# A fused Mamba and mixture-of-experts kernel on one core: a reordered tail, with gated products on GpSimd

## The reference

```python
h = concat([cls, patchify(x) @ W.T + b]) + pos          # then the text tokens behind it
# layer 2 (Mamba): h -> LN -> xz = h @ W_in ; causal conv ; silu ; delta, B, C ; scan over time
y = ys + xc * D
h2 = h + (y * silu(z)) @ W_out                           # "output projection"
# layer 3: a shared gated FFN over all rows, and experts for the 512 rows of an index
shared = LN(silu(x1) * x2) @ sw3.T + sb3
x_moe = x[index_b, index_t]
scores = sigmoid(x_moe @ eg_w.T + eg_b); top1 = argmax(scores + exp_bias)
h1 = einsum('md,ehd->meh', x_moe, ew1) + eb1
h2 = einsum('md,ehd->meh', x_moe, ew2) + eb2
z  = LN(silu(h1) * h2)
out = einsum('meh,edh->med', z, ew3) + eb3               # all 8 experts; the top one is taken
final.at[index_b, index_t].set(shared_w * shared + expert_w * out[top1])
```

## Time and profile before

| | |
|---|---|
| median of 3 runs | 1708.54 us (1707.23 to 1710.84) |
| profiled execution | 1710.15 us |
| its span in the trace | 1708.0 us |
| busy: TensorE, VectorE, ScalarE, GpSimd | 87%, 90%, 78%, 92% of the span |
| last scan of the loop begins | at 1620.44 us |
| last TensorE instruction begins its group | at 1699.34 us |

### The profile page before, as it was taken

How to read it: one execution, slowest core, us unless ns; L and a number is a source line. 1 busy time by engine, 2 the same in 40 slices (tenths; PEclk the granted TensorE clock), 3 DMA queues, 4 the chain that set the end, 5 groups by cost and what they waited for, 6 DMA issues and landing times.

```text
span 1708.0 us, 28038 instructions
## 1 busy us (share of the span) xinstructions
PE 1483.6 (87%) x9868; PEld 1065.3 (62%) x9868; DVE 1544.3 (90%) x1389; ACT 1328.5 (78%) x3100; POOL 1563.2 (92%) x782
## 2 busy tenths in 40 slices
PE   8778898899889988898888898988988889896688
PEld 7656666666666666666666666666666666664355
DVE  2499999999999999999999999999999999999944
ACT  2577788888888888888888888888888888887644
POOL 0599999999999999999999999999999999999914
PEclk8888999999999999999999999999999999997899
DMA  4667755566667555666665556666655566566110
GB/s 136 143 126 178 182 127 124 121 133 140 136 137 152 125 124 117 137 142 138 135 153 125 121 120 137 142 137 136 153 125 122 123 133 142 121 143 140 39 35 16
DMA packets 194430, 218.47 MB, mean 128 GB/s; under 512 B 94011, under 2 KB 184773, under 8 KB 193778
## 3 DMA queue, kind: packets, MB, share of 16 engines
q1 hardware_dynamic: 193522, 215.51, 56.9%
q0 software_dynamic: 576, 1.17, 0.3%
q10 hardware_dynamic: 192, 0.01, 0.0%
HBM read 169.92 MB, written 47.09 MB: 127 GB/s over the span
## 4 chain that ended last, share of the span: by engine, by line
DVE 24%; POOL 19%; ACT 18%; issue 13%; PE 12%; DMA 12%; SPq 2%; DVEq 0%; ACTq 0%; POOLq 0%
DVE psum L1317 12%; POOL xr L1664 12%; ACT psum L1020 7%; DMA u<-u_scratch 7%; DVE xr L1317 5%; DVE xr L1326 5%; PE psum L620 4%; DMA u_scratch<-u 4%; POOL u L1685 3%; ACT L1142 2%; POOL xr L1672 2%; ACT L1051 2%; PE psum L792 2%; SPq L482 2%; ACT soft L1068 2%
## 5 line engine op out<-in xcount | busy, mean ns | idle before, releaser
L1664 POOL TENSOR_TENSOR xr<-u,bbc 128x912 f32<-128x912 f32 x512 | 1076.3, 2137 | 13.7 <-DMA u<-u_scratch 13.7
L1020 ACT ACTIVATE psum<-delta,a_neg 128x228 f32<-128x228 f32 x2048 | 804.9, 440 | 199.4 <-DVE xr L1326 159.3
L1317 DVE TENSOR_TENSOR_SCAN psum<-psum,xr 128x912 f32<-128x912 f32 x320 | 654.3, 2045 | 10.6 <-POOL xr L1664 7.4
L1672 POOL TENSOR_TENSOR xr<-xr,cbc 128x912 f32<-128x912 f32 x192 | 409.3, 2132 | 35.7 <-DVE xr L1317 32.7
L1317 DVE TENSOR_TENSOR_SCAN xr<-psum,xr 128x912 f32<-128x912 f32 x192 | 393.3, 2048 | 31.3 <-ACT psum L1020 31.3
L1326 DVE TENSOR_TENSOR xr<-psum,cbc 128x912 f32<-128x912 f32 x320 | 352.2, 1101 | 3.8
L721 PE MATMUL psum<-xr,fold 128*32 128x228 f32 x4096 | 294.7, 385 | 30.3 <-POOL xr L1672 16.6
L620 PE MATMUL psum<-xh,win 128*128 128x228 f32 x1024 | 222.9, 367 | 41.0 <-ACT xs L1051 31.6
L620 PEld LDWEIGHTS psum<-xh,win 128*128 128x128 f32 x1024 | 192.6, 193 | 68.4 <-ACT xs L1051 41.9
L671 PE MATMUL psum<-xi,conv_d 128*128 128x228 f32 x1024 | 211.2, 358 | 0.0
L671 PEld LDWEIGHTS psum<-xi,conv_d 128*128 128x128 f32 x1024 | 190.5, 189 | 16.3 <-issue 11.7
(11 more groups left out here) (204 smaller groups left out, 1590.4 us busy)
## 6 DMA issues: line engine op xcount, KB each, us to landing
delta<-delta_scratch SPq DMA_DIRECT2D x256, 228.0 KB, 6.6
u<-u_scratch SPq DMA_DIRECT2D x256, 228.0 KB, 4.4
bbc<-bc_scratch SPq DMA_DIRECT2D x128, 114.0 KB, 2.6
u_scratch<-u SPq DMA_DIRECT2D x64, 228.0 KB, 4.1
cbc<-bc_scratch SPq DMA_DIRECT2D x128, 114.0 KB, 2.8
delta_scratch<-delta SPq DMA_DIRECT2D x64, 226.0 KB, 6.3
out<-ob SPq DMA_DIRECT2D x32, 228.0 KB
h_scratch<-h SPq DMA_DIRECT2D x31, 228.0 KB
```

Of the source, the lines that this page charges most:

```text
L1020: ins = nc.scalar.activation(slot(k)[:, j * TOK:(j + 1) * TOK], delta4[:, c // 2, j, c % 2], ACT.Exp, scale=a_neg[:, c, j, n:n + 1])
L1317: nc.vector.tensor_tensor_scan(x if k in on_pool(i) else slot(k), slot(k), x, 0.0, ALU.mult, ALU.add).then_inc(scan_done, 1)
L1664: nc.gpsimd.tensor_tensor(xr[:, k % XRING], u4[:, c // 2, :, c % 2], bbc[:, p, n].unsqueeze(1).to_broadcast([P, J, TOK]), ALU.mult).then_i ...
L1672: nc.gpsimd.tensor_tensor(xr[:, k % XRING], xr[:, k % XRING], cbc[:, p, k % NI].unsqueeze(1).to_broadcast([P, J, TOK]), ALU.mult).then_inc ...
```

## The change

The last output projection becomes two parts: `out_first` (behind unit 13 of group 31) and `out_second` (where `out_proj` was), in bank CB. The feed-forward work of group 31 goes to bank BB. `bias_rows` goes ahead of unit 10 into bank BB, and VectorE's addition to it goes from `after_last` to behind unit 12. TensorE's, VectorE's and ScalarE's orders of the expert part are rewritten. `gated` of blocks 0 to 2 goes from VectorE to GpSimd, where `shared_rows` goes ahead of `rstd_of(0)`.

```diff
-            h2_ps = psum[0:T, AB, 0:SEQ * DM].rearrange("p (s d) -> p s d", s=SEQ)
+            def h2_ps(g):
+                return psum[0:T, CB if g == GROUPS - 1 else AB, 0:SEQ * DM].rearrange("p (s d) -> p s d", s=SEQ)
...
-                return {GROUPS - 2: 2, GROUPS - 1: 3}.get(g, AB)
+                return {GROUPS - 2: 2, GROUPS - 1: BB}.get(g, AB)
...
+                    def out_first():
+                        g = GROUPS - 1
+                        pe.wait_ge(sz_done, 2 * GROUPS)
+                        pe.wait_ge(y_done, CH // 2 * g + 1)
+                        for s in range(SEQ):
+                            for k in range(DC):
+                                pe.matmul(h2_ps(g)[:, s, k * P:(k + 1) * P], h0[:, g % HRING, k, s * T:(s + 1) * T], ident[:],
+                                          start=(s == 0 and k == 0), stop=False)
+                            for c in range(CH // 2):
+                                pe.matmul(h2_ps(g)[:, s], y[:, g % 2, c, s * T:(s + 1) * T], wout[:, c], start=False, stop=False)
+                    def out_second():
+                        g = GROUPS - 1
+                        pe.wait_ge(y_done, CH // 2 * GROUPS)
+                        for s in range(SEQ):
+                            for c in range(CH // 2, CH):
+                                mm = pe.matmul(h2_ps(g)[:, s], y[:, g % 2, c, s * T:(s + 1) * T], wout[:, c],
+                                               start=False, stop=(s == SEQ - 1 and c == CH - 1))
+                        mm.then_inc(h2_mm, 1)
...
 (h2_turn)
+                        if g == GROUPS - 2:
+                            pe.wait_ge(eb3_done, 1)
...
 (v_center)
-                        elif g == GROUPS - 3:
-                            pe.wait_ge(h2_ev, GROUPS)
...
 (bias_rows)
-                        pe.wait_ge(sz_done, 2 * GROUPS)
+                        pe.wait_ge(x2t_ev, GROUPS - 2)
-                            mm = pe.matmul(psum[0:E, CB, 0:DM], ...
+                            mm = pe.matmul(psum[0:E, BB, 0:DM], ...
...
 (after_last, PE)
-                        out_proj(GROUPS - 1)
+                        out_second()
...
 (body, PE)
-                            if i == GROUPS - 1 and k == 13:
+                            if i == GROUPS - 1 and k == 10:
                                 bias_rows()
                             if runs(i):
                                 reduce_states(i, k)
+                            if i == GROUPS - 1 and k == 13:
+                                out_first()
...
 (gates)
-                        if m == 0:
-                            pe.wait_ge(eb3_done, 1)
 (hidden)
+                        pe.wait_ge(xmt_ev, m + 1)
-                            pe.wait_ge(o_done, GROUPS)
+                            pe.wait_ge(o_done, GROUPS - 1)
...
 (PE, the experts)
                     turn_rows(0)
                     ffn_out(ga)
+                    hidden(0, 0)
                     v_center(gz)
-                    turn_rows(1)
-                    hidden(0, 0)
-                    v_var(gz)
-                    turn_rows(2)
-                    turn_rows(3)
-                    ffn_out(gz)
+                    for m in range(1, MT):
+                        turn_rows(m)
                     for m in range(MT):
                         gates(m)
+                    v_var(gz)
                     hidden(0, 1)
                     hidden(1, 0)
+                    ffn_out(gz)
+                    hidden(1, 1)
                     turn_hot()
-                    hidden(1, 1)
                     hidden(2, 0)
                     hidden(2, 1)
                     turn_out(0)
...
 (ACT, the experts)
+                    rows_copy(1)
                     v_square(gz)
-                    rows_copy(1)
                     expert_rstd(3)
-                    ln3_rstd(gz)
                     rows_copy(2)
                     rows_copy(3)
-                    out_copy(gz)
+                    ln3_rstd(gz)
...
                     nc.scalar.activation(wts[:], two[:], ACT.Exp).then_inc(gate_act, 1)
+                    out_copy(gz)
                     gate_silu(0)
...
                     affine(0)
                     gate_silu(2)
+                    affine(1)
                     zt_copy(0)
-                    affine(1)
                     gate_silu(3)
-                    for m in range(1, MT):
-                        zt_copy(m)
-                        if m + 1 < MT:
-                            affine(m + 1)
+                    affine(2)
+                    zt_copy(1)
+                    affine(3)
+                    zt_copy(2)
+                    zt_copy(3)
...
 (DVE)
+                    def expert_bias():
+                        dve.wait_ge(eb_in, EB_IN)
+                        dve.wait_ge(eb3_mm, 1)
+                        nc.vector.tensor_tensor(eb3x, psum[0:E, BB, 0:DM], eb3r, ALU.add).then_inc(eb3_done, 1)
...
 (after_last, DVE)
-                        dve.wait_ge(eb_in, EB_IN)
-                        dve.wait_ge(eb3_mm, 1)
-                        nc.vector.tensor_tensor(eb3x, psum[0:E, CB, 0:DM], eb3r, ALU.add).then_inc(eb3_done, 1)
...
 (body, DVE)
                                 times_c(i, p, k)
+                            if i == GROUPS - 1 and k == 12:
+                                expert_bias()
...
 (DVE, the experts)
                     expert_rows(3)
-                    v_norm(gz)
+                    bias_of(0, 0)
                     choose(...)              # the seventeen steps, unchanged
-                    bias_of(0, 0)
+                    v_norm(gz)
                     bias_of(0, 1)
-                    gated(0)
+                    bias_of(1, 0)
                     stats(0)
-                    for m in range(1, MT):
-                        bias_of(m, 0)
-                        bias_of(m, 1)
-                        gated(m)
-                        stats(m)
+                    bias_of(1, 1)
+                    bias_of(2, 0)
+                    stats(1)
+                    bias_of(2, 1)
+                    bias_of(3, 0)
+                    stats(2)
+                    bias_of(3, 1)
+                    gated(3)
+                    stats(3)
...
 (POOL)
+                    def gated(m):
+                        pool.wait_ge(at_done, m + 1)
+                        pool.wait_ge(a_done, 2 * m + 2)
+                        nc.gpsimd.tensor_tensor(a1[:, m], at[:, m % 2], a2[:, m % 2], ALU.mult).then_inc(ev_done, 1)
+                    gated(0)
+                    shared_rows()
                     rstd_of(0)
+                    gated(1)
                     rstd_of(1)
-                    shared_rows()
+                    gated(2)
                     rstd_of(2)
                     shared_part()
                     rstd_of(3)
```

More of the change, by code:

```diff
@@ L1567, in _ @@
                     expert_rows(3)
-                    v_norm(gz)
-                    steps = [0]
-                    def choose(ins):
-                        steps[0] += 1
-                        ins.then_inc(gate_step, 1)
-                        dve.wait_ge(gate_step, steps[0])
-                    dve.wait_ge(gate_mm, MT)
-                    dve.wait_ge(gw_in, GW_IN)
-                    choose(nc.vector.tensor_tensor(sc[:], psum[:, CB, 0:MT * (1 + E)].rearrange("p (m e) -> p m e", m=MT),
-                                                 gb[:].unsqueeze(1).to_broadcast([P, MT, 1 + E]), ALU.add))
@@ L1581, in _ @@
-                    dve.wait_ge(gate_act, 1)
-                    choose(nc.vector.tensor_scalar(sc[:], sc[:], 1.0, None, ALU.add))
-                    choose(nc.vector.reciprocal(sc[:], sc[:]))
-                    choose(nc.vector.tensor_tensor(biased[:], sc[:, :, 1:], xb[:].unsqueeze(1).to_broadcast([P, MT, E]), ALU.add))
-                    choose(nc.vector.tensor_reduce(best[:], biased[:], AX.X, ALU.max))
-                    choose(nc.vector.tensor_tensor(hot[:], biased[:], best[:].unsqueeze(2).to_broadcast([P, MT, E]), ALU.is_equal))
@@ L1587, in _ @@
-                    dve.wait_ge(pool_c, 5)
-                    choose(nc.vector.tensor_tensor(hot[:], hot[:], prio[:].unsqueeze(1).to_broadcast([P, MT, E]), ALU.mult))
-                    choose(nc.vector.tensor_reduce(best[:], hot[:], AX.X, ALU.max))
-                    choose(nc.vector.tensor_tensor(hot[:], hot[:], best[:].unsqueeze(2).to_broadcast([P, MT, E]), ALU.is_equal))
-                    choose(nc.vector.tensor_tensor(biased[:], hot[:], sc[:, :, 1:], ALU.mult))
-                    choose(nc.vector.tensor_reduce(two[:, :, 1:2], biased[:], AX.X, ALU.add))
@@ L1593, in _ @@
-                    choose(nc.vector.tensor_copy(two[:, :, 0:1], sc[:, :, 0:1]))
-                    choose(nc.vector.tensor_reduce(best[:], two[:], AX.X, ALU.max))
-                    choose(nc.vector.tensor_tensor(two[:], two[:], best[:].unsqueeze(2).to_broadcast([P, MT, 2]), ALU.subtract))
-                    dve.wait_ge(gate_act, 2)
```

(34 more changed lines are left out.)

13 lines of the change are left out of this document (6 added, 7 removed).

## The result

The changed kernel took 1723.2 us, the median of four runs from 1719.4 to 1725.9, against 1709.1 before: 14.1 us more. The ratio, worked out from all runs, is 1.0073 (95% interval 1.0053 to 1.0093), less than that of the two medians (1.0083); it is worth 12.5 us. Slower, as forecast (0.85). By the median, the 1718.1 was 5.1 too low and the range, which ended at 1723.0, misses by 0.2; by the ratio, 1708.5 would become 1721.0, inside it. The profiled execution is the lowest of the four, 1719.4, with a span of 1717.5.

What follows compares the result with a forecast made beforehand. Waits in each engine's fixed order, from the last group on, bound the kernel. 6.0 - 2.7 = 3.3, + 3.1 to silu 0, + 3.9 to rstd_of(0), - 1.7, + 1.0: 9.6 on 1708.5 gives 1718.1 us, range 1712 to 1723.

Steps and rivals of the forecast that it cites:

- Step 1: Last group of the loop: VectorE waits for bias rows before scan 13, making y_out 6.0 us late.
- Step 2: Last output projection: only 8 weight instructions remain behind y_out, first part hidden; saves 2.7 us, copy 3.3 late.
- Step 3: From rows_copy(0) to gates and choice: TensorE's and ScalarE's new orders leave the second gate exponential 2.1 us late.
- Step 4: ScalarE before the experts: silu 0 waits behind out_copy(31) and the table load; 6.4 us late, 3.1 of it new.
- Rival B: ScalarE pauses after the table load, making silu 0 and all behind it 0.67 us later: 1718.8 us; chance 0.04.
- Step 5: GpSimd in the expert blocks: gated products and gathers make rstd_of(0) 10.3 us late, rstd_of(3) 8.6; rounds of 7.6.
- Step 6: End of the experts: turn_out(2) waits for zt_copy(1), 9.6 us late, then 15.0 us on TensorE as before.
- rival A: TensorE's clock falls in the tail after longer idle times: 1720 to 1724 us; chance 0.20.
- Rival C: A smaller loss: stall before scan 13 half recovered, or gathers cost less on GpSimd; 1712 to 1715 us; chance 0.15.
- Rival D: VectorE's relief sets the time in the four expert blocks, three saving 3.7 us: 1702 us; chance 0.09.
- Rival E: Gains and losses meet if stall and gathers both fail to reach the end: within 3.4 of 1708.5 us; chance 0.06.

Runs made afterwards that it cites:

- front_stalled: Kernel before with divided projection, its banks and bias rows ahead of unit 10, VectorE's bias addition behind unit 12; experts as before: ratio 1.0026 to the kernel before.
- gathers_first: Kernel before, only the four gathers of shared rows moved ahead of rstd_of(0): ratio 0.9995 to the kernel before.
- bias_late: Changed kernel with VectorE's bias-row addition moved from behind unit 12 to behind unit 15: 1719.4 us, ratio 1.0051 to the kernel before.
- kept_busy: Changed kernel with throwaway products on TensorE ahead of hidden(2,1), turn_out(0) and turn_out(2): ratio 1.0080 to the kernel before.
- mended: Changed kernel: bias addition behind unit 15, out_copy(31) behind silu 0, gathers in pairs, zt_copy(1), (2) ahead of affine(2), (3): 1711.1 us, ratio 0.9992 to before.
- mended_on_vector: As mended, but three gated products back on VectorE and gathers in pairs behind rstd_of(0) and rstd_of(1): ratio 0.9999 to the kernel before.
- front_alone: Kernel before with divided projection, its banks and bias rows ahead of unit 10, VectorE's bias addition behind unit 15; experts as before: ratio 1.0002 to the kernel before.
- copy_and_gathers: Changed kernel with out_copy(31) behind silu 0 and shared-row gathers in pairs behind gated(1) and gated(2): ratio 1.0059 to the kernel before.

## Why the prediction was right, and what it mis-sized

**Step 1, the stall: right** in place and kind. VectorE's loss at y_out is 6.2 us where unit 8 runs at 1.2 GHz (front_stalled; 6.0 forecast). In the changed kernel's profile, where it runs at 2.4, it is 3.5, or 4.3 against gathers_first, which has no stall and unit 8 at 2.4 too (13.1). I took the low clock of the one trace for granted; six of the eight profiled kernels with the stall had it low.

**Step 2, the divided projection: right in the changed kernel, wrong as a gain of its own.** That the first part is hidden, since it goes "while TensorE waits for units 14 and 15", holds only under the stall of step 1. Without it, the bound that I named, up to 2.9, is the case: 2.7 measured, all that the division saves. With both, the net of 3.3 came out (3.6 in front_stalled); in the changed kernel's profile it is 0.9, by the shorter stall.

**Step 3: right.** From turn_rows(0) to the end of the choice, the changed kernel gains 1.1 us on before (1.2 forecast).

**Step 4: right.** From turn_rows(0), silu 0 is 3.1 us late (3.1 forecast), with the table load of 1.28 between copy and silu and no pause on either side. The pause of 1.38 us that the Trainium skill (ScalarE: Activation LUTs, What ACT_TABLE_LOAD costs) adds isn't there: silu begins at 1662.98, load's end 1662.97. Rival B is out.

**Step 5: right, mis-sized by 0.6.** rstd_of(0) follows silu 0 by 8.4 us (9.0 forecast), since the four gathers take 4.9 us, not 5.5. Their first takes 0.99 with no gated product of VectorE beside it, 2.14 before with one; so the collision was real. It speaks against what the Trainium skill (SBUF — State Buffer, Who interferes with whom) infers for descriptor writing. Even by my own rows the 5.5 was too high: 6.40 less the 1.19 is 5.2. Rounds took 7.6, 8.1 and 5.5 us (7.65, 7.65 and 5.8 forecast). In the second, bias_of(3,0), ahead of stats(2) on VectorE, waited 3.34 us for hidden(3,0) behind the transposes of 1.97 us; in bias_late, where those took 1.09, the round took 7.5. GpSimd's product took 2.35.

**Step 6: the term that was missing.** turn_out(2) is 8.0 us later than before (9.6 forecast), but from there to the end it takes 17.8 us, not the 15.0 that I carried over at full clock. That is rival A. I had it as a case of its own with 0.20; it came with the forecast's waits rather than in their place, since the waits lengthen the idle times. In kept_busy's profile it is gone. The granted clock is low at 1636 us too (0.66), and the time between the copy and turn_rows(0) is 1.3 us longer than before.

Together: 9.6 forecast; add the low clock at the end, 2.8, and in the first feed-forward work, 1.3, and take off 0.6 for the gathers: 13.1, against 12.5 to 13.7 by the two ratios. No profile shows this sum. In that of the changed kernel the 9.6 shrinks, since the stall cost 2.4 less at the copy than forecast, and 10.8 came out. kept_busy, the same kernel with unit 8 at 1.2 GHz, is at 102.6 with its tail at the full clock, 10.4 behind before; the 2.9 that separate its tail from the changed kernel's (14.9, 17.8) would make it 13.3. It had nothing extra at 1636 us and 1.7 ahead of silu 0 instead. So where the low stretches fall differs between executions, and that the profiled span (1717.5, 1717.6 forecast) fits so well is luck: it began its last group 1.6 us earlier than that of before, the stall came out smaller, and the clock cost more.

Rival C's first half did happen in both profiles of the changed kernel (bias rows at the full clock), but its time of 1712 to 1715 didn't, as the clock took it back later. Rival D, a relief of VectorE that counts, is out: mended and mended_on_vector are the same within their intervals. Rival E needed the stall and the gathers to fail to reach the end; bias_late shows the stall in the time, while the gathers' part is seen only in profiles.

## What to carry to other kernels

A reordering by hand must be read per queue: for each moved instruction, what stands behind it, and when what it waits for is ready; here the repair of four such places took back all the loss, while the ideas of the change brought no measurable gain (divided projection, front_alone 1.0002; early gathers, gathers_first 0.9995; products on GpSimd, mended against mended_on_vector). Work put "into an idle time" ahead of the critical sums must fit into it, or be put behind them. Waits of TensorE can cost twice: in all seven profiles with the longer ones a low stretch of its clock followed and cost 1.4 to 3.1 us, though the timing didn't show that cost by itself.

## What was not expected of the hardware

- Two engines can hold each other up both ways: a gated product of VectorE beside GpSimd's subtraction took 2.09 us, 1.23 alone; GpSimd's small product (L1782) beside a gated product of VectorE 0.69 (1.28 in the kernel before), 0.20 alone.
- The same loop had unit 8's skip product at 0.65 or at 1.13 us; 3 of 14 profiles had it at 0.65. In those three a part of group 30's projection had taken 3.2 to 3.4 us in place of 1.89, and the idle time ahead of the product was 2.7 us in place of 4.40. So the low stretch wasn't absent but had come earlier, where VectorE's loop hid it. One trace doesn't tell which clock a stretch gets.
- A gap of 2.6 us ahead of turn_out(2) went with a transposition at 1.94 us, in place of 1.04 to 1.09. With gaps of 2.60 and 2.67 in copy_and_gathers and bias_late it took 1.06, and the low stretch began behind it.
- A gather that begins during a gated product of VectorE took 2.13 to 2.14 us (three profiles) or 1.47 and 1.49 (two), in place of 0.94 to 1.10. In gathers_first one that began 0.01 us behind such a product took 0.94, and the product 1.27.
